# Last norm of a two-layer GNN kernel: ScalarE's square two steps later, VectorE's sum of squares two steps behind its add

## The reference

```python
edge_index = jnp.stack([src, dst])
x = _layernorm(x + _L0_gnn_ref(x, edge_weight1, edge_index, ...), axis=-1)
x = _layernorm(x + _L1_gnn_ref(x, edge_weight, edge_attr_3, edge_index, ...), axis=-1)
```

## Time and profile before

| what | us |
|---|---|
| median of 3 runs | 2194.02 (2193.39 to 2197.69) |
| the profiled execution | 2183.9 |
| its span, first to last instruction | 2182.1 |
| last stage in it: first DMA issue of `first_rows` | at 2020.6 |
| last `scale_4` begins | at 2173.28 |
| busy over the span: PE 61%, POOL 58%, DVE 50%, ACT 29% | |

### The profile page before, as it was taken

The page is one execution under the profiler, slowest core; times in us unless marked ns, Lnnn a source line. Parts: engine busy times, 40 slices in busy tenths (PEclk is TensorE's granted clock), DMA queues, the critical chain, the costliest instruction groups (busy, mean ns, idle before and its releaser), DMA issues.

```text
span 2182.1 us, 23911 instructions
## 1 busy us (share of the span) xinstructions
PE 1327.2 (61%) x6086; PEld 947.4 (43%) x6086; DVE 1097.1 (50%) x3121; ACT 626.7 (29%) x1642; POOL 1256.4 (58%) x1315
## 2 busy tenths in 40 slices
PE   5644454332316655333332368999959999999564
PEld 4322242111204444233321355666627777777554
DVE  9543552332322222343432264777746777777565
ACT  0000000000001111000000495666624444442775
POOL 6466676666665656666667411333368888882243
PEclk8555555555558877566665698999969999999665
DMA  1011011111115555344431454454422333333675
GB/s 32 21 30 29 26 30 30 30 31 29 30 46 159 150 153 157 107 113 125 126 99 47 112 152 106 149 160 150 143 74 54 93 94 93 94 93 93 154 192 143
DMA packets 330295, 204.59 MB, mean 94 GB/s; under 512 B 32299, under 2 KB 318704, under 8 KB 330160
## 3 DMA queue, kind: packets, MB, share of 16 engines
q1 hardware_dynamic: 269008, 140.38, 24.2%
q0 software_dynamic: 35280, 49.84, 8.0%
q10 hardware_dynamic: 25872, 12.85, 2.0%
HBM read 124.03 MB, written 78.92 MB: 93 GB/s over the span
## 4 chain that ended last, share of the span: by engine, by line
PE 46%; issue 20%; DVE 12%; another core or an unknown queue 11%; POOL 4%; DVEq 2%; DMA 2%; SPq 1%; ACT 1%; ACTq 0%; POOLq 0%
PE bank L878 10%; PE bank L848 6%; PE bank L871 6%; DVE res L1083 5%; PE bank L757 3%; PE bank L801 3%; PE bank L756 3%; PE bank L811 3%; PE bank L803 2%; DVE oh L951 2%; PE bank L841 2%; PE bank L839 2%; PE bank L887 2%; PE bank L855 2%
## 5 line engine op out<-in xcount | busy, mean ns | idle before, releaser
L462 POOL DMA_INDIRECT placed<-pay,pos_i x392 | 395.5, 1009 | 305.8 <-issue 288.1
L457 POOL DMA_INDIRECT gat<-in_x,key_i x392 | 395.5, 1009 | 126.5 <-issue 116.8
L811 PE MATMUL bank<-woh,pw 128*128 128x128 f32 x784 | 149.9, 362 | 258.3 <-DVE woh L1062 170.3
L756 PE MATMUL bank<-oh,lower 128*128 128x196 bf16 x392 | 126.5, 341 | 296.2 <-issue 148.5
L1083 DVE TENSOR_TENSOR res<-res,bank 128x128 f32 x588 | 168.9, 287 | 266.0 <-remote 78.8
L504 POOL DMA_INDIRECT gat<-x_d,src_i x196 | 256.9, 1311 | 58.9 <-issue 52.0
L982 DVE SCALAR_TENSOR_TENSOR junk<-iota,w_f,bank 128x196 f32<-128x196 f32 x392 | 148.7, 417 | 247.5 <-remote 116.5
L811 PEld LDWEIGHTS bank<-woh,pw 128*128 128x128 f32 x784 | 136.1, 266 | 271.7 <-issue 249.2
L878 PE MATMUL bank<-prod,ident 128*128 128x280 f32 x896 | 218.2, 402 | 0.0
L756 PEld LDWEIGHTS bank<-oh,lower 128*128 128x128 bf16 x392 | 44.1, 113 | 378.9 <-issue 284.6
L878 PEld LDWEIGHTS bank<-prod,ident 128*128 128x128 f32 x896 | 171.8, 192 | 46.8 <-issue 0.6
(11 more groups left out here) (146 smaller groups left out, 2419.9 us busy)
## 6 DMA issues: line engine op xcount, KB each, us to landing
pw<-placed SPq DMA_DIRECT2D x588, 68.0 KB, 2.0
pw<-placed SPq DMA_DIRECT2D x98, 272.0 KB
xin<-in_x_t SPq DMA_DIRECT2D x98, 256.0 KB
hot_d<-woh SPq DMA_DIRECT2D x49, 256.0 KB
x_d<-res POOLq DMA_DIRECT2D x49, 256.0 KB, 3.8
oh<-hot_d SPq DMA_DIRECT2D x28, 448.0 KB
placed<-pay SPq DMA_DIRECT2D x28, 448.0 KB
out<-out ACTq DMA_DIRECT2D x49, 256.0 KB, 2.7
```

What stands on the lines that cost most here:

```text
L457: pool.indirect_dma_start(gat[:, t, :], None, x, bass.IndirectOffsetOnAxis(ap=key_i[:, 1 - c, t:t + 1], axis=0)).then_inc(s_gat[n // CHUNK ...
L462: pool.indirect_dma_start(placed[c].rearrange("t p r -> (t p) r"), bass.IndirectOffsetOnAxis(ap=pos_i[:, c, t:t + 1], axis=0), pay[i % 4][ ...
L756: pe.matmul(column(k), lower[:, :], oh[:, t, :], start=True, stop=False)
L811: ins = pe.matmul(quarter(bank, k), pw[i % 6][:, k, 0:P], woh[i % 3][:, k, :], start=True, stop=True)
```

## The change

The square of a batch is issued two steps later on ACT, and the sum of squares two steps later on DVE. The buffer of the squares gets a third copy, and ACT waits for the sum of three batches ago, where it was two. `scale_4` and `store_4`, which follow the norm, also move by two steps, so their distance to `square_4` is what it was.

```diff
-        sq4 = ring(sb, "sq4", 2, [P, BC])
+        sq4 = ring(sb, "sq4", 3, [P, BC])
...
-            staged([apart_4] + [None] * 7 + [scale_4], NB)
+            staged([apart_4] + [None] * 9 + [scale_4], NB)
...
             def square_4(b):
                 act.wait_ge(z_y, b + 1)
-                wait(act, z_ssq, b - 1)
-                act.activation(wins(sq4[b % 2][:, :]), batch(b), ACT.Square, scale=D ** -0.5).then_inc(z_sq, 1)
+                wait(act, z_ssq, b - 2)
+                act.activation(wins(sq4[b % 3][:, :]), batch(b), ACT.Square, scale=D ** -0.5).then_inc(z_sq, 1)
...
-            staged([away_from_4, hot_4, None, square_4] + [None] * 5 + [store_4], NB)
+            staged([away_from_4, hot_4, None, None, None, square_4] + [None] * 5 + [store_4], NB)
...
             def norm_4(b):
                 dve.wait_ge(z_sq, b + 1)
-                dve.tensor_reduce(ssq4[four % 2][:, o:o + G * J], nodes(sq4[b % 2][:, :]), AX_X, ALU.add).then_inc(z_ssq, 1)
+                dve.tensor_reduce(ssq4[four % 2][:, o:o + G * J], nodes(sq4[b % 3][:, :]), AX_X, ALU.add).then_inc(z_ssq, 1)
...
-            staged([add_4, norm_4], NB)
+            staged([add_4, None, None, norm_4], NB)
```

## The result

The changed kernel took 2182.99 us (median of 6 runs, 2181.47 to 2186.91), the kernel before beside it 2197.49 us (6 runs, 2193.39 to 2198.74). The ratio is 0.9943 with a 95% interval of 0.9932 to 0.9953: 0.57% or 12.5 us faster (the two medians lie 14.5 us apart). The prediction said 13.5 us and 0.62% less; the time lies in its range.

The account below looks back on a forecast made before the run. The prediction took the line of square, sum, newton, add and next square to bound the last stage. SP's pace (-15.6 us) and a longer end (+2.1) sum to -13.5 us, median 2180.5, range 2172 to 2191.

Parts of the forecast that it names:

- What bounds the kernel before: Last stage: square, sum, newton, add and next square lie in one line, 2.85 us a batch from the twelfth batch on.
- The wait of 2.46 us goes: ACT's idle time before each fourth square, waiting for DVE's add, vanishes with some 1.8 us to spare.
- SP at 2.49 us a batch is next: SP's DMA issues set the last stage's pace after the change: first to last away 119.6 us, 15.6 us less.
- The end of the stage: From last away to last scale, DVE's sums still owed cost +2.1 us, possibly 1 to 4: last scale at +15.3.
- One block in each newton, which changes nothing at SP's pace: One POOL scale meeting DVE's newton adds up to 1.05 us: loop 2.51 us a batch, still SP's pace.
- Transfers set the pace: Rival, last stage: a DMA share of 0.81 as ceiling, 2.64 us a batch, -6 us, 2188; chance 0.13.
- Nothing gained: Rival: two POOL scales meet each newton on DVE, 2.78 us a batch, 0 us, 2194; chance 0.08.
- slower: Rival: three scales meet every newton on DVE, 3.04 us a batch, +13 us, 2207; chance 0.04.
- The median: Whole kernel: runs' median taken as 10.1 us above the profiled execution, as before; changed kernel's span 2168.6, median 2180.5 us.

Follow-up runs that it names:

- e2: The kernel before, with each last-stage batch loaded by one DMA from fixed tiles instead of four; ratio to before 0.9982, pace 133.5 us.
- e3: ACT's part of the change alone, with DVE's sum of squares one step behind its add as in the kernel before; ratio to before 1.0026.
- e1: The changed kernel, with each last-stage batch loaded by one DMA from fixed tiles instead of four; ratio to before 0.9865, pace 106.1 us.
- e12: e9 with both queues loading all four tile numbers into registers, using three and one; ratio to before 0.9885, pace 109.4 us.
- e8: The changed kernel with POOL's scale on 2 of the 32 features; ratio to before 0.9934, end of the stage 13.9 us.
- e5: The changed kernel measured again, on the chip of later runs; ratio to before 0.9944, pace 121.2 us, end of the stage 16.7 us.
- e6: The changed kernel with the shift of square, sum, scale and store cut from two steps to one; ratio to before 0.9932, end 14.8 us.
- e4: DVE's part of the change alone, with ACT's square three steps behind away as in the kernel before; ratio to before 0.9968.
- e9: e6 with ACT issuing the load of each batch's fourth window behind the four away instructions, SP the other three; ratio to before 0.9922.
- e7: e6 with ACT issuing the loads of each batch's third and fourth windows behind its one-hot, SP the first two; ratio to before 1.0090.

## Why the prediction was right, point by point

- **What bounds the kernel before.** Right. The line of square, sum, newton, add and square was the limit: e2 relieves SP and changes little, e3 keeps DVE's order and with it 34.6 us of wait. Misread was from when on: the prediction let the line rule from the twelfth batch, but the fifth square already waits, and the next long step comes 11.40 us later, as at pace. The 2.49 us of the first 15 batches are SP's alone, which runs ahead into its six buffers.

```profile
2042.80 0.63 ACT L690 ACTIVATE sq<-res 128x512 f32<-128x512 f32 x1 [2.35 <-DVE res L1214]
...
2054.20 0.63 ACT L690 ACTIVATE sq<-res 128x512 f32<-128x512 f32 x1 [2.46 <-DVE res L1214]
```

- **The wait of 2.46 us goes.** Right: 31.9 us became nothing; the 3.1 us that squares still wait are for sums.
- **SP at 2.49 us a batch is next.** Right: 119.6 us were predicted for the pace, 119.8 came, and e1 and e12 show that it falls as soon as SP has less to do.
- **The end of the stage.** The term was mis-sized: +2.1 us predicted, +3.5 measured. What the working left out is that newton is held up by scales here, and counted from the last away at 2154.16 the rows show where. The newton beside it, which began at 2154.09, ended at +3.6 instead of +3.1, its first instruction taking 1.08 us instead of 0.20. The root of batches 44 to 47 came at +10.9 instead of +10.2 and the fourth scale behind it at +14.7 instead of +14.1. The last scale was to follow that one at once, at +15.3. It came at +16.7, after 0.94 us of waiting for the last newton, which the working had off the path. That newton took 5.09 us (2165.69 to 2170.78), with four stretched instructions; unblocked it takes 2.26 (e8). So 0.7 us of the missing 1.4 were there when the root of 44 to 47 came, and 0.7 came from the last newton. e8 shortens the scale and gets 2.7 us of the end back, part of it the shorter scales themselves.
- **One block in each newton, which changes nothing at SP's pace.** Right in number and in effect (at most one block, e8 no faster in pace), wrong in which instruction it mostly strikes. I had given the two-input instructions a maximum near 1 us all through; their mean stayed at 225 ns, and the one struck was newton's first, with one input. Which one is struck depends on the spacing of the work: in e5 one two-input instruction took 1.10 us (at 1932.95), and in e6, with one step, the first instruction's mean is 366 ns, while those of two two-input ones rise to 246 and 250. The Trainium skill (SBUF — State Buffer, section "SBUF: two separate sides") names, beside two-input instructions, those in a 2-port performance mode, which tensor_scalar can enter, and I had left this half of its rule out. By it all eleven instructions can be blocked and not nine. The trace agrees for the first and second (0.93 us at 2093.55, 0.97 at 2166.25); the mode they ran in no trace here shows.
- **Transfers set the pace.** Fell: at a share of 0.83 nothing queued (stores landed in 2.7 us in the median as before, loads in 2.2 after 2.1), and e1 ran at 0.95.
- **Nothing gained, and slower, by two and three blocks.** Didn't occur: no newton of a full group met two scales. Three and more blocks came only in the last newton.
- **The median.** It was carried over from one execution, as 10.1 us above it. That execution proved the shortest of its kernel by 9.5 us; the changed one's profiled execution lay 1.5 us below its median. But this offset was only taken over from the kernel before, so it cancels: the forecast is 2194.0 less 13.5. It lies 2.5 us below the measured time because the median of before itself rose by 3.5 us with three more runs, less 1.0 by which the medians fell more than forecast. The difference between the kernels, which is what was worked out, doesn't hang on either. That the time itself came within 2.5 us is partly luck, as the executions of before lie 5.3 us apart.

## What to carry to other kernels

Where an instruction of a late batch stands in an in-order queue behind one of an earlier batch that waits on another engine, count the loop in steps of the fastest engine, and move both ends of it: moved alone, either end only shifts the wait (e3, e4). Move by no more than the loop needs, as each step lengthens the end of the stage (e6). And look for the next pace before the edit: an issue queue that shows no wait, like SP here, can be the limit that decides what the edit is worth.

## What the runs showed of the hardware that was not expected

- The load of tile numbers into registers took 300 ns for four, 682 for three (e9) and 816 for two (e7, medians on SP; in e7 both queues loaded at once), 391 for one (e9, on ACT's queue) and 520 for four (e12, on ACT's queue, while SP's took 302). What sets the time isn't shown.
- A DMA issued on ACT's queue costs ACT no time where it has instructions in hand (the store: in e1 steps of 2.21 us before the first store and with it) and leaves ACT idle where its queue has just waited (e7: 1.07 us in the step shown).
- POOL's scale of 1.05 us stretched an instruction of DVE with one input as well (0.93 us for 0.20), but lengthened neither the sum of squares (682 ns in the mean with 686 before) nor the add from PSUM (678 and 678).
